# Chain between convolution attention and token keys: halves, earlier slots, four score pairs moved, block counts from a table

## The reference

```python
x = _L0_conv_ref(x, ...)                     # 8 images, 128 channels, 32 x 32 = 1024 positions
t = _to_tokens(x)
t = t + _L1_attn_ref(_ln_t(t), w_qkv)        # 8 heads of 16
t = t + _L1_ffn_ref(_ln_t(t), ...)           # top 2 of 8 experts, 128 -> 512 (gelu) -> 128
x = _from_tokens(t, x)

# inside _L0_conv_ref, per image
x = group_norm(hidden_states, pre_g, pre_b) + pos_emb
spatial_enhanced = x * sigmoid(conv(silu(conv3x3(silu(conv(x))))))
sh = group_norm(x, norm_g, norm_b)           # as tokens
standard_out = softmax(qh @ kh.T / 4) @ vh   # 8 heads of 16, q, k, v from sh
parts = [softmax(qm @ km.T / 8) @ vm ...]    # 2 heads of 64, qm from spatial_enhanced
fused = silu(concat(standard_out, parts) @ ff_w1.T + ff_b1) @ ff_w2.T + ff_b2
final = fused @ out_w.T + out_b
return group_norm(final, post_g, post_b) + residual
```

## Time and profile before

| | us |
|---|---|
| median of 3 runs | 3449.59 |
| lowest, highest | 3449.12, 3455.41 |
| the profiled execution | 3450.68 |
| its span, first to last instruction | 3448.8 |
| PE busy | 2944.1 (85%) |
| DVE busy | 2244.8 (65%) |
| ACT busy | 1703.8 (49%) |
| POOL busy | 634.3 (18%) |

### The profile page before, as it was taken

One profiled execution on the slowest core, in us unless ns is written; L12 is line 12 of the kernel. 1 busy time (PEld: TensorE's weight loads), 2 busy tenths in 40 slices (PEclk: granted clock), 3 DMA queues, 4 the chain that ended last, 5 costly groups with the idle time before them and its releaser, 6 DMA issues. The chain is left out here.

```text
span 3448.8 us, 43859 instructions
## 1 busy us (share of the span) xinstructions
PE 2944.1 (85%) x15646; PEld 1220.4 (35%) x15646; DVE 2244.8 (65%) x4177; ACT 1703.8 (49%) x2519; POOL 634.3 (18%) x558
## 2 busy tenths in 40 slices
PE   3789898998889898898889888898989988898945
PEld 1225322262224432262223522253322622244325
DVE  4664877467774778557684777648784677747740
ACT  1355365545555365554555455553655455553613
POOL 3010321014010220103220220102210140102222
PEclk9799899999999899998999999998999999998967
DMA  4014330173103530163102721144301631035324
GB/s 101 1 49 143 72 63 12 40 193 57 26 14 123 127 62 3 49 178 68 30 14 74 176 50 14 46 141 77 63 12 40 192 59 26 14 123 127 62 71 136
DMA packets 171534, 252.19 MB, mean 73 GB/s; under 512 B 26323, under 2 KB 80287, under 8 KB 171215
## 3 DMA queue, kind: packets, MB, share of 16 engines
q1 hardware_dynamic: 162127, 230.65, 26.6%
q0 software_dynamic: 9216, 18.89, 2.2%
HBM read 192.59 MB, written 56.86 MB: 72 GB/s over the span
## 5 line engine op out<-in xcount | busy, mean ns | idle before, releaser
L1285 DVE TENSOR_REDUCE blockmax<-ps 128x1 f32<-128x512 f32 x1656 | 1094.2, 685 | 391.0 <-PE ps L683 381.0
L1106 ACT ACTIVATE prob<-ps 128x1024 f32<-128x1024 f32 x1024 | 997.1, 1021 | 587.1 <-PE ps L859 576.8
L683 PE MATMUL ps<-ks,qs 96*128 96x512 bf16 x1656 | 655.7, 408 | 176.2 <-DVE blockmax L1285 120.4
L859 PE MATMUL ps<-qs,ks 99*128 99x512 bf16 x2048 | 625.5, 395 | 10.5 <-DMA qs<-maxrow_dram 7.5
L683 PEld LDWEIGHTS ps<-ks,qs 96*128 96x128 bf16 x1656 | 161.4, 101 | 856.4 <-DVE blockmax L1285 682.4
L1150 ACT ACTIVATE prob<-ps,b1t 128x128 f32<-128x128 f32 x828 | 235.8, 368 | 187.0 <-PE ps L958 183.7
L576 POOL TENSOR_TENSOR rs<-vn,vec 128x1 f32<-128x1 f32 (+1 forms) x43 | 42.8, 996 | 1454.7 <-DVE vn L1234 990.9
L859 PEld LDWEIGHTS ps<-qs,ks 99*128 99x128 bf16 x2048 | 196.5, 101 | 266.5 <-issue 73.3
L873 PE MATMUL ps<-prob,va_b 128*32 128x512 f32 x2048 | 288.4, 637 | 0.0
L1296 DVE TENSOR_REDUCE blockmax<-ps 128x2 f32<-128x1024 f32 x224 | 263.7, 1220 | 30.7 <-PE ps L719 27.2
L873 PE MATMUL ps<-prob,va_a 128*32 128x512 f32 x2048 | 283.0, 625 | 0.0
(11 more groups left out here) (227 smaller groups left out, 3470.6 us busy)
## 6 DMA issues: line engine op xcount, KB each, us to landing
shared<-in_w SPq DMA_DIRECT2D x108, 256.0 KB, 3.4
prob<-in_w SPq DMA_DIRECT2D x108, 256.0 KB, 3.7
parts_dram<-parts SPq DMA_DIRECT2D x34, 768.0 KB, 5.1
ks<-parts_dram SPq DMA_DIRECT2D x204, 128.0 KB, 4.5
qs<-parts_dram SPq DMA_DIRECT2D x204, 128.0 KB, 7.3
routed<-in_w SPq DMA_DIRECT2D x90, 256.0 KB, 3.6
xe<-in_w SPq DMA_DIRECT2D x54, 256.0 KB, 3.1
oatt<-in_w SPq DMA_DIRECT2D x54, 256.0 KB, 3.6
```

What stands on the lines that cost most here:

```text
L683: pe.matmul(ps[:, MX + n % 2, :], qs[0:ROWS, slot, h, tile * P:(tile + 1) * P], ks[0:ROWS, slot, h, cols(k)], start=True, stop=True).then_ ...
L859: mm = pe.matmul(ps[:, SC + h, :], ks[:, slot_of(a, g), h, t * P:(t + 1) * P], qs[:, slot_of(a, g), h, cols(q)], start=True, stop=True)
L1106: act.activation(prob[:, n % 3, 2 * pr:2 * pr + 2, :], ps[:, SC + 2 * pr:SC + 2 * pr + 2, :], ACT.Exp, scale=HD ** -0.5).then_inc(exp_done ...
L1285: dve.tensor_reduce(blockmax[:, unit_of(j), cell_of(j), k:k + 1], ps[:, MX + n % 2, :], AX.X, ALU.max).then_inc(blocks_used[f], 1)
```

## The change

1. **Pairs.** `PAIR_SLOT` goes from 16 to 14, `B_EARLY` and `A_FRONT` from 56 to 48. There are 24 pairs, 22 in slots and two after the last. The 8 `b` blocks that leave the pairs go to the token stage (80 `b`, 48 `a0` blocks there), and 8 `a0` blocks become `a1` blocks of the convolution stage (112). The unread products (L996) go. `turn_b_0` stands behind pair 16, tg5 behind pair 6.
2. **Chain.** ff1, ff2, outp, post, tr_x, tr_nb, kB, qB are handed over in halves of 512 columns. Their slots are nearer to each other, and vB's copy goes from DVE to ACT.
3. **Sums first.** In the last step of each parts half the ones products come before the value products, and DVE's reciprocal waits for the sums alone.
4. **Tables.** `CONV_BLOCKS` and `TOKEN_BLOCKS` give the blocks of every step. km0, km1, qm0, qm1 go from steps 1 to 4 to steps 16 to 19. The turns and later smalls stand one to two steps later.
5. **Queues.** POOL takes the next image's pre `rs` between the gathers and the weighting. SP takes the rows of `b` unit 2 before the queries' first group.

```diff
-A_FRONT = 56
-B_EARLY = 56
+A_FRONT = 48
+B_EARLY = 48
-CONV_WINDOW = {0: ["tro0"], 1: ["tro1", "km0"], 2: ["tro2", "km1"], 3: ["turn_a1_1", "tro3", "qm0"], 4: ["qm1"],
+CONV_WINDOW = {0: ["tro0"], 1: ["tro1"], 2: ["tro2"], 3: ["tro3"], 5: ["turn_a1_1"], 6: ["trn0"], 7: ["trn1"],
+               8: ["logits"], 9: ["tra0"], 12: ["slots"], 13: ["turn_a1_2"], 16: ["km0"], 17: ["km1"],
...
+EXPERT_WINDOW = {1: ["ff1"], 2: ["ff2"], 3: ["outp"], 4: ["tg2", "post"], 7: ["tr_x"], 8: ["tg3"], 10: ["tr_nb"],
+                 11: ["kB"], 12: ["tg4", "qB"], 13: ["vB"], 17: ["tg5"], 25: ["turn_b_0"]}
...
+CONV_BLOCKS = (3, 3, 3, 3, 4) + (4,) * 8 + (5, 5, 4, 5, 4, 5, 4) + (4,) * 8 + (0,) * 4
+TOKEN_BLOCKS = (4,) * 4 + (3, 3, 4, 4, 4, 4, 5, 5) + (4,) * 20
+HALVES = {"ff2": ("ff_act", "ff2_half"), "outp": ("ff2", "outp_half"), "tr_x": ("xr", "trx_half"),
+          "tr_nb": ("ln_b", "trn_half"), "kB": ("xh_b", "kb_half"), "qB": ("xh_b", "qb_half")}
-PAIR_SLOT = 16
+PAIR_SLOT = 14
-EARLY_TURN = 19
+TURN_PAIR = UNIT // 2
+ROWS_PAIR = 6
...
-            at = (MX, SC, SC + 2)[(d - UNDER_EXPERTS) % 3]
+            at = (SC, SC + 2, MX)[(d - UNDER_EXPERTS) % 3]
...
                 spread_parts(0, 1)
+                if token:
+                    spread_max("b", 2)
                 spread_group(0, 1, 0)
                 if token:
-                    spread_max("b", 2)
                     spread_max("b", 3)
...
+                if token:
+                    rstd("pre_rstd", 1)
                 pool.wait_ge(rows_gathered, 16 * ROUTES)
...
+                elif name in HALVES:
+                    before, event = HALVES[name]
                     for h in range(2):
+                        pe.wait_ge(done[before], h + 1)
...
+                            mm = pe.matmul(ps[:, pair_bank(h), :], weight, src[:, cols(h)], start=True, stop=True)
+                        if h == 0:
+                            mm.then_inc(done[event], 1)
...
+                        pe.wait_ge(mexp_done, n)
+                        if t == NT - 1:
                             for m in range(MULTI):
                                 mm = pe.matmul(ps[MD * m:MD * (m + 1), MX, :], w("ones")[:, 0:MD], tile[:, m, :],
                                                start=False, stop=True)
+                            mm.then_inc(sums_done, 1)
...
+                            d = SLOT_PAIRS * (s - PAIR_SLOT) + i
+                            if d < UNDER_EXPERTS:
+                                early_pair(d)
+                            if d in (ROWS_PAIR, TURN_PAIR):
+                                pe.wait_ge(blocks_used["b"], 2 * d)
+                                small_product("turn_b_0" if d == TURN_PAIR else "tg5")
                 if token:
                     for d in range(UNDER_EXPERTS, B_EARLY // 2):
                         early_pair(d)
-                        if d == EARLY_TURN:
-                            pe.wait_ge(blocks_used["b"], 2 * UNDER_EXPERTS)
-                            small_product("turn_b_0")
-                        if d >= EARLY_TURN:
-
-                            pe.matmul(ps[:, OB, 0:384], w("ident"), xh[:, 0:384], start=True, stop=True)
...
-                    read_small(two(ta[:, :]), pair(), name, "ff2", ACT.Identity, bias=v("ff_b2"))
+                            act.activation(ta[:, cols(h)], src, ACT.Identity, bias=v("ff_b2")).then_inc(done["ff2"], 1)
...
+                elif name == "vB":
+                    act.wait_ge(small_full, small[name])
+                    for h in range(2):
+                        ins = act.activation(v_cols[1][:, 4 * h:4 * h + 4, :, 0:HD],
+                                             ps[:, pair_bank(h), :].rearrange("p (t h d) -> p t h d", t=4, h=NH), ACT.Copy)
+                    ins.then_inc(small_free, 1)
...
             def take_multi(q):
 
+                dve.wait_ge(sums_done, q + 1)
+                link(dve.reciprocal(rec[:, :], ps[:, MX, :]))
                 dve.wait_ge(mpv_done, NT * (q + 1))
-                link(dve.reciprocal(rec[:, :], ps[:, MX, :]))
```

More of the change, by code:

```diff
@@ L90 @@
 CONV_EXTRA = {4: ["stats_e"], 5: ["norm_e"], 10: ["routes"], 14: ["gates"]}
 PARTS_WINDOW = {2: ["tra3"], 4: ["tob0"], 6: ["tob1"], 12: ["tg0"], 14: ["tg1"]}
[L92 to L96, removed]
@@ L105, with turns_of @@
 UNDER_EXPERTS = SLOT_PAIRS * (SLOTS - PAIR_SLOT)
[L108 to L112, removed]
+def turns_of(counts, blocks):
+    ends = [sum(counts[:n + 1]) for n in range(len(counts))]
+    assert ends[-1] == len(blocks)
+    return [blocks[end - count:end] for end, count in zip(ends, counts)]
 def conv_blocks(n):
-    return [("a1", j) for j in blocks_at(n, 0, 26, A_FRONT, ALL_BLOCKS)]
+    return turns_of(CONV_BLOCKS, [("a1", j) for j in range(A_FRONT, ALL_BLOCKS)])[n]
 def token_blocks(n, token):
+    late = [("a0", j) for j in range(A_FRONT)]
     if not token:
-        return [("a0", j) for j in blocks_at(n, 11, 18, 0, A_FRONT)]
-    return ([("b", j) for j in blocks_at(n, 0, 18, B_EARLY, HEAD_BLOCKS)]
-            + [("a0", j) for j in blocks_at(n, 18, 14, 0, A_FRONT)])
+        return turns_of((0,) * 16 + (4,) * 12 + (0,) * 4, late)[n]
+    return turns_of(TOKEN_BLOCKS, [("b", j) for j in range(B_EARLY, HEAD_BLOCKS)] + late)[n]
 def unit_of(j):
@@ L869, in weigh_values @@
                 if a == 1 and n == 0:
-                    pe.wait_ge(done["v_b"], 1)
+                    pe.wait_ge(small_free, small["vB"])
                 for j in range(GH):
@@ L943, in tensor_program @@
                                                start=False, stop=True)
+                            mm.then_inc(sums_done, 1)
+                        for m in range(MULTI):
+                            mm = pe.matmul(ps[MD * m:MD * (m + 1), (OB, MX + 1)[q], :], vm[:, t, MD * m:MD * (m + 1)],
+                                           tile[:, m, :], start=(t == 0), stop=(t == NT - 1))
                         mm.then_inc(mpv_done, 1)
@@ L1427, in small_product @@
                 elif name == "ff1":
-                    dve.wait_ge(done["tanh_ff"], 1)
-                    dve.tensor_scalar(two(tb[:, :]), pair(), v("ff_b1"), 0.5, ALU.add, ALU.mult).then_inc(small_free, 1)
-                    freed(name)
-                    dve.scalar_tensor_tensor(out=tb[:, :], in0=ta[:, :], scalar=1.0, in1=tb[:, :],
-                                             op0=ALU.add, op1=ALU.mult).then_inc(done["ff_act"], 1)
+                    for q in range(2):
+                        dve.wait_ge(done["tanh_ff"], q + 1)
+                        ins = dve.tensor_scalar(tb[:, cols(q)], ps[:, pair_bank(q), :], v("ff_b1"), 0.5, ALU.add, ALU.mult)
+                        if q == 0:
+                            link(ins)
+                        else:
+                            ins.then_inc(small_free, 1)
+                            freed(name)
+                        dve.scalar_tensor_tensor(out=tb[:, cols(q)], in0=ta[:, cols(q)], scalar=1.0, in1=tb[:, cols(q)],
+                                                 op0=ALU.add, op1=ALU.mult).then_inc(done["ff_act"], 1)
                 elif name == "outp":
-                    dve.wait_ge(done["outp"], 1)
-                    dve.sem_inc(small_free, 1)
-                    group_stats(tb, "post")
+                    group_stats(tb, "post", "outp")
                 elif name == "post":
@@ L1455, in small_product @@
                     i = "kq".index(name[0])
-                    dve.wait_ge(done[f"{name[0]}1_b"], 1)
                     if i == 1:
                         dve.wait_ge(done["k3_b"], 1)
-                    dve.tensor_tensor(two(rem[:, :]), pair(), two(parts[:, i, 0, :]), ALU.subtract).then_inc(small_free, 1)
+                    for hh in range(2):
+                        dve.wait_ge(done[f"{name[0]}1_b"], hh + 1)
+                        ins = dve.tensor_tensor(rem[:, cols(hh)], ps[:, pair_bank(hh), :], parts[:, i, 0, cols(hh)],
+                                                ALU.subtract)
+                        if hh == 0:
+                            note(ins)
+                        else:
+                            ins.then_inc(small_free, 1)
                     freed(name)
```

153 lines of the change are left out of this document (79 added, 74 removed).

## The result

The changed kernel takes 3421.6 us (median of 5, 3414.4 to 3429.4), the kernel before 3449.6 (5 runs). The ratio is 0.9916, 95% interval 0.9904 to 0.9929: faster by 0.8%, 28 us. The forecast was 85.

A forecast was written before the change was run, and what follows sets the result against it. PE, busy for 85%, was the engine to look at, with DVE the bound in part of the convolution stage. Terms sum to - 9.6 us per image, x 8 = - 77, and prologue - 8: - 85, so 3365 us (range 3318 to 3405).

The forecast's parts named there:

- token stage: Stage after the tail: 129.5 us taken for 132.6, with some 3 us less waiting at the turns, - 3.1 per image.
- tail: From last expert product to first token scores: four pairs left in place of ten, 6.6 us, a gain of 13.1.
- (a): Convolution steps 0 to 5 lose km0, km1, qm0, qm1 and one block each: about - 8.4 us per image.
- (e): Convolution stage: turn_a1_1 sits closer to step 8, + 0.7 us per image.
- (c): Three of convolution steps 13 to 18 hold five blocks, where DVE is the bound: + 1.9 us per image.
- (d): Convolution step 16: PE stands some 5.4 us for turn_a1_2's rows, split behind the slots chain; + 4.4 us per image.
- (b): The four small products return in convolution steps 16 to 19, and steps 26 and 27 hold multi pairs: + 5.1 us.
- T: The end of the last expert product in an image, from which the prediction counts times in tail and token stage.
- The rival built on it, 3470: Without unread products PE idles behind the last expert product and in step 16, staying at 1.2 GHz: 3470 us, chance 0.04.
- transfers hold the start: Token stage starts 11 us after the last expert product because rows or loads are late: 3400 us, chance 0.11.
- the chain doesn't keep up: Expert stretch: every chain link stalls PE, and the stretch grows by 7 in place of 2.4: 3402 us, chance 0.05.
- The rows of turn_a1_2 cost nothing: Convolution step 16: PE arrives later, or the stall covers work DVE owes anyway: 3330 us, chance 0.18.

The follow-up runs named there:

- e5: Changed kernel with POOL waiting for x1 before it weights the gathered rows: 3408.1 us, ratio 0.9867.
- e6: Changed kernel with rs computed by POOL between the 14th and 15th gather, not behind the 16th: 3397.8 us, ratio 0.9838.
- e12: Changed kernel with rs put back behind POOL's weighting and additions: 3462.1 us, ratio 1.0042.
- e1: Changed kernel with turn_a1_2 ahead of the slots chain, so its rows go out sooner: 3400.7 us, ratio 0.9841.
- e9: Changed kernel with the four pairs moved back (56 early blocks) and 8 blocks fewer in the convolution stage: 3445.3 us, ratio 0.9988.
- e3: Kernel before without its nine unread products in the tail: 3452.5 us, ratio 1.0001.
- e8: Changed kernel with four unread products behind the last pair: 3422.9 us, ratio 0.9911.
- e10: Changed kernel with four pairs moved back, rows of turn_a1_2 first, rs between gathers and weighting, weighting behind x1: 3361.5 us, ratio 0.9748.

## Why the prediction was wrong

The means per image, in us; the column "forecast" is the prediction's.

| step | forecast | measured |
|---|---|---|
| tail | - 13.1 | - 13.2 |
| expert stretch | + 2.4 | + 2.7 |
| ff1, sums first | - 0.5 | - 1.2 (image 4: parts 0.5, ff1 0.8) |
| convolution, (a) and (e) | - 7.7 | - 5.3 |
| convolution, (c) and (d) | + 6.3 | + 6.3 |
| convolution, (b) | + 5.1 | + 5.6 |
| token stage | - 3.1 | + 1.7 |
| prologue, once | - 8 | - 4 |

The three convolution rows are taken between the value products of steps 1, 9, 18 and 32, so km0 and km1 of (b), in steps 16 and 17, lie in the row of (c) and (d). Eight whole iterations took 3.5 us per image less (the rows sum to - 3.4), where - 9.6 was forecast (- 10.6, and 1.0 for the clock, which the measured rows hold). 8 x 6.1, the prologue's 4, less 4.5 that the work behind the last image gave, are 48 of the 49 us between the forecast and the profiled execution.

- **The step that failed is the token stage**, "I take 129.5, the best image today, for 132.6: - 3.1". It came out at 134.4, and that is 4.8 of the 6.1 us. I placed `rs` right (T + 24.8 said, T + 24.4 measured) but asked only when it comes, not what x1 then stands beside, and I had DVE ready for it 2.6 us too late. Its old place had x1 run behind POOL's work, its new one beside it. e5 and e6 show the price, 17 and 27 us. e6 brings back 2.8 of the 4.8 in the stage itself. What holds the other 2.0 isn't shown. The clock is one candidate: the stage's time at half clock, about 22 us for about 14 before, lies in its first nine steps, and no run separates it from DVE's work there. Without the move it is 43 us worse (e12), so "most of the tail's gain would be lost" was right in its sign and too strong: 5.4 of 13.2 an image.
- **The second half of that term had no ground.** "Some 3 us less waiting" of the turns apart from norm and c20 did not show: from step 9 on, where c20 stands, the token stage took 86.3 before and 86.8 after. The turn beside norm lies ahead of that, in the part that grew. And the earlier trace rows were of the worst image: 4.0 us above the 0.7 that every wait for `rs` has, where the mean of the eight is 1.2.
- **(d) was right as a stall and its size** (5.4 said, 5.16 measured). Its price was too high: 4.4 charged, 2.8 in the stretch and 3.2 an image in the time by e1. That the row of (c) and (d) comes out at + 6.3 as forecast is luck: without the stall it is still + 3.5, where (c) had + 1.9. What I did not see is that it would pin the stage, so that a saving just ahead of it turned into waiting (e9). (a)'s shortfall isn't that, since the stretch from step 1 to 9 stays at 34.1 to 35.4 us in every version with this table, with the rows first too. There DVE's statistics and norm of e, the turn and the blocks meet behind step 5 (distances of 6.4 and 5.3 to 7.5 us). The term (a) was over-sized by about 2.4: I took each small product's price off, and part of it may have been cover for that work, which no run here tests.
- **(b) came near for no good reason.** Its terms are 3.6 and 1.2 and 3.0, that is 7.8; the 2.7 taken off for "a turn's small surplus" stand in no row. Measured behind step 18: 5.6.
- **The clock** went from 0.94 to 0.93 over the span. The convolution stages of the changed kernel spread with it (129.2 us at 0.96, 133.2 at 0.91). The rival built on it, 3470, did not come. The rule of the Trainium skill (TensorE: Matmul & The Clock Gate, "Why this matters for your kernels") that the prediction weighed, that gaps between bursts of matmuls bring half rate back, agrees with e3 and e8: without such products the token stage's clock is 0.92, with them 0.95 and 0.94. Yet the unread products brought nothing: the totals of e3 and e8 did not move, while the wait for `rs` took up the difference.
- The rivals "transfers hold the start" and "the chain doesn't keep up" fell by the tail's 6.5 and the stretch's 68.3. "The rows of turn_a1_2 cost nothing" fell by the stall in all eight images and by e1.
- The 2 us for each transfer come from a section of the Trainium skill (DMA: Bandwidth & Descriptors, "Anatomy of one DMA") that is written for transfers issued by GpSimd. SP issues these; the rows of this case, 1.40 and 2.34, carried the sum.
- **The prologue** gave 4 of 8. In e9, with 8 blocks more, it is 9.7 longer than in the changed kernel, so the blocks were worth what was said or more, and the rest of the change costs some 6 us there (by difference). Where, no run shows.

What stays open, then, is how much of the token stage's last 2.0 us and of (a)'s 2.4 us is clock and how much DVE: no kernel here kept one and changed the other.

## What to carry to other kernels

When an operation is moved earlier, list what runs on every engine at its new place, not only whether its inputs are there: here VectorE's small operations and its passes over 128x1024 in SBUF were held beside GpSimd's arithmetic. A wait on a late transfer can swallow what is saved just ahead of it; take it away before weighing anything that saves time in front of it, since e9 and e10 give opposite answers to one question. The same goes for a test of the clock: in front of a wait, what a better clock gives is waited away. And read a wait as the sum over all images by its line, for one engine alone, before taking one image's row as a term.

## What the runs showed of the hardware

Beside a GpSimd operation on 128x1024 float32 a VectorE operation on 128x1 took 1.55 and 1.85 us (0.15 alone; 1.47 to 1.65 in the eight images of the changed kernel), a 128x1024 one with two tensors 2.40 and 3.02 (1.28), one with a single tensor 2.23 (0.74), a 16x128 cast 1.82 (0.21), while reductions of 128x512 from PSUM kept 0.68 and the statistics of 128x512 (one input, in SBUF) 0.67. GpSimd's two additions took 6.08 in place of 4.82. GpSimd's issue of gathers did not hold VectorE: `nb` and `vn` beside it took 0.15. A float32 product of 384 columns is recorded as two passes and took 0.67 us at full clock. Four of them in front of the token stage raised that stage's granted clock from 0.92 to 0.94.
